# Moving the second transposed unit of the next batch's rows from the middle of a step to its end

## The chip, the cores and the metric

The kernel runs on one core of one Trainium2 chip. The metric is the device time of one execution in microseconds, the median of the runs. TensorE (PE) multiplies and transposes through PSUM banks, VectorE (DVE) and ScalarE (ACT) read those banks and write to SBUF, GpSimd (POOL) multiplies probabilities and sends rows, and SyncE (SP) starts the other transfers. Each engine works off its own program in order. Semaphores are the only order between them.

## The reference

Four blocks are chained, each as x = x + layernorm(block(layernorm(x))), on 8 batches of 512 rows by 256 features, in f32:

- block 1: causal attention with 16 heads of 64 and a linear position bias, then an output projection;
- block 2: a matrix product with a pooled low-rank term, here folded into one weight;
- block 3: a linear attention with two key and value sets, an inner layernorm and an output projection;
- block 4: a shared gated network plus 64 experts, of which each row takes 8.

The attention of block 1 is what matters here:

```
scores = einsum('bihd,bjhd->bhij', q, k) * scale + bias      # causal, 16 heads
attn   = softmax(scores);  out = einsum('bhij,bjhd->bihd', attn, v) @ Wo + bo
```

q, k and v are products of the normalised rows of x with weights. TensorE contracts over partitions, so the normalised rows `xa` (128 rows by 256 features, four tiles) must first be transposed into `xT` (128 features by 512 rows, two chunks of features).

## The kernel before, in words

The first half of the program (to about 1140 us) goes through the batches. Batch 0 is written out, batches 1 to 6 are a hardware loop, and batch 7 is written out again. The second half does the experts and the rest.

A batch is eight steps, g = 1 to 7 and then 0. A step scores the pair of heads g, normalises its softmax, and finishes the pair before: its probabilities are transposed and multiplied with the values. It also projects q and k of the next pair. Blocks 2 to 4 of the batch before (`TENSOR_AT`, `SCALAR_AT`, `VECTOR_AT`) and the preparation of the next batch (`X_AT`, `RING_AT`) are laid into slots of these steps. Step 7 projects pair 0 of the next batch, for which it needs all of the next batch's `xT`.

The order of TensorE within a step is written out in `TENSOR_STEP`, and that of ScalarE in `SCALAR_STEP`:

```
TENSOR_STEP: P0 b S0 S1 q T00 P1 T01 T02 T10 T11 k T12 S2 O e
SCALAR_STEP: F03 F13 P0 b q E00 T00 E01 P1 T01 T02 T10 T11 k E02 T12 E10 E11 E12 O e
```

P are the projections (L1551), S the scores (L1562), T the transposes of probabilities (L1573; T11 is the second unit of the second head, T12 the third), O is the product with the values (L1587), E and F are exponentials on ScalarE (L804). b, q, k and e are the slots. O stands last but one.

P, T, O and the units of `RING_AT` share PSUM banks 4 and 5 in turn. TensorE fills one bank while ScalarE empties the other. A unit may start once the unit two turns before it has been copied out by ScalarE (`ring_free`, L1517, on semaphore `ring_ready`). T02 and T10 borrow score banks instead and take no turn. ScalarE takes the copies in the same order, waiting for each unit on `ring_psum`.

The units of `RING_AT` are V (values of the next batch, L1542), L (transposes for block 3, L1620) and X. X 0 and X 1 are the two chunks of the next batch's `xT`: four 128x128 transposes each on TensorE (L1533, which wait for the normalised rows of DVE, L1067) and one copy of 128x512 by ScalarE (`a_copy` at L788). They stand in batches 0 to 6, seven times in all.

Two orders at a slot matter. TensorE's `extras` issues the units of the slot first and then the parts of `TENSOR_AT`. ScalarE's `extras` takes the parts of `SCALAR_AT` first and then the units. At slot e of step 6 the part is `l1o_T` in both: eight transposes into banks 6 and 7 (L1610) and two copies to `xTp`. In batch 0 no such part exists. The first thing of step 7 on TensorE is P0, and for the next batch's pair it waits for the copy of X 1:

```
if nxt[1] == 0:
    pe.wait_ge(ring_ready, ring_count(a, ("X", 1)))
projection(a, ("P", g, int(part[1])), nxt[1], int(part[1]))
```

The first copy of O goes to `oT`, those of T to `pT`. All of them are made by the helper at L788, so the rows tell them apart by what they write.

Of the kernel before, what the change touches and what calls it, by code (L numbers as in the profile page):

```python
# [79 lines left out]
def bass_sandwich(nc, x, wq, wk, wv, wo, bo, ffn_w, ffn_d, l1_wq, l1_wqT, l1_bq, l1_wk, l1_bk, l1_wv, l1_bv,  # L80
# [12 lines left out]
    with ctx:  # L93
# [184 lines left out]
        def score_banks(hp, u):  # L278
# [16 lines left out]


        RING_AT = {(1, 'b'): (('V', 4),), (1, 'k'): (('V', 5),), (3, 'k'): (('V', 6),), (4, 'b'): (('V', 7),), (5,
                   'k'): (('L', 0),), (6, 'b'): (('L', 1),), (6, 'k'): (('X', 0), ('X', 1)), (7, 'k'): (('V', 0), ('V',
                   1)), (7, 'e'): (('V', 2),), (0, 'e'): (('V', 3),)}
        EARLY_RING = (("X", 0), ("X", 1), ("P", 0, 0), ("P", 0, 1), ("V", 0), ("V", 1), ("P", 1, 0), ("V", 2),  # L300
                      ("P", 1, 1), ("V", 3))
# [1734 lines left out]
```

How the kernel before makes its waits and increments, by code:

```python
        @block.sync  # L463
# [20 lines left out]
                for dst, src in ((a_q[:, :, D], l1_bq), (lng_c[:], ln_g), (lnb_c[:], ln_b)):  # L484
                    sp.dma_start(dst, src.rearrange("(c p) -> p c", p=P)).then_inc(post_loaded, 16)
            def load_xs(a):
                sp.wait_ge(xs_used, at(a, 1, 0))
                sp.dma_start(xs[:], x_v[index(a)]).then_inc(xs_loaded, 16)
            load_xs((None, 1))
            sp.wait_ge(setup_made, N_MADE)
            slots_v = disp.rearrange("(e c) w -> c e w", c=CAP)
            for rows, t in ((slots_v[0:P], 0), (slots_v[P:CAP], 1)):
                n = rows.shape[0]
# [8 lines left out]
            def batch_out(p):  # L506
                sp.wait_ge(x3_ready, at(p, 1, 1))
                sp.dma_start(x3_d[index(p)], x2[:].rearrange("p t d -> p (t d)")).then_inc(batch_stores, 16)
                sp.wait_ge(xTp_ready, at(p, C * ROUNDS, C * ROUNDS))
                sp.dma_start(hT_d[index(p)], hT[:].rearrange("p c n -> p (c n)")).then_inc(batch_stores, 16)
                sp.wait_ge(batch_stores, at(p, 32, 32))
                sp.sem_inc(stored, 1)
# [1 line left out]
            def next_x(a, p):  # L515
                sp.wait_ge(x1_used, at(p, 1, 1))
                sp.dma_start(x1[:], x_v[index(a)]).then_inc(x1_loaded, 16)
# [17 lines left out]
            last = (None, B - 1)
            sp.wait_ge(ring_psum, ring_count(last, ("P", HP - 2, 1)))
            for n in range(3):
# [10 lines left out]
                load_w1(e, e)  # L550
                load_w2(e, e)
            sp.wait_ge(x1_used, B)
            load_early(EARLY - 1)
```

## Time and profile before

| | us |
|---|---|
| median of 3 runs | 2179.06 |
| the three runs | 2185.43, 2179.06, 2171.68 |
| profiled execution, its time | 2178.4 |
| profiled execution, its span | 2176.3 |
| TensorE busy in the span | 2081.0 (96%) |
| ScalarE busy | 825.8 (38%) |
| VectorE busy | 941.5 (43%) |
| GpSimd busy | 846.0 (39%) |
| mean granted clock of TensorE | 0.98 |

The span runs from the first to the last instruction. A granted clock of 1.00 is 2.4 GHz and 0.50 is 1.2 GHz. "Idle before" in a row is the time for which the engine did nothing before the group, with the engine and line that ended it; "issue" and "remote" mean that the profile shows no engine that did.

### The profile page before, as it was taken

The numbers are of one execution on the slowest core, as the hardware profiler recorded it, in microseconds if no ns is written. First come the engines' busy times: TensorE is split into PE (matmuls) and PEld (weight loads), VectorE is DVE, ScalarE is ACT, GpSimd is POOL, SyncE is SP. The second block draws the span as 40 slices with busy tenths as digits, with TensorE's granted clock in tenths as the row PEclk, the third lists the DMA queues.
The fourth block names the chain that finished last, engine by engine and source line by source line (L and its number), as shares of the span: only waits on it lengthen the run. The fifth ranks groups of instructions, "written<-read, shape, count | busy, mean of one in ns | idle before, by whom it ended". The sixth has DMA issues, their size and how long they took to land.

```text
span 2176.3 us, 37551 instructions
## 1 busy us (share of the span) xinstructions
PE 2081.0 (96%) x11788; PEld 1540.6 (71%) x11788; DVE 941.5 (43%) x3719; ACT 825.8 (38%) x2130; POOL 846.0 (39%) x958
## 2 busy tenths in 40 slices
PE   9999999999999999999999699799999999999998
PEld 4565565565655655655666466399999999999956
DVE  3436564565564665655656324022222222222236
ACT  5756556545555465555564011111111111111110
POOL 3427436447265265274472503203222232222232
PEclk9999999999999999999999799799999999999999
DMA  6800001000000000000004000078878778778841
GB/s 211 232 1 11 11 31 66 34 22 26 31 22 10 31 16 11 23 20 13 16 29 182 24 10 32 21 273 264 262 267 269 254 264 274 263 251 276 290 107 65
DMA packets 101726, 245.65 MB, mean 113 GB/s; under 512 B 22412, under 2 KB 78187, under 8 KB 93240
## 3 DMA queue, kind: packets, MB, share of 16 engines
q1 hardware_dynamic: 75448, 224.09, 28.4%
q0 software_dynamic: 26112, 19.55, 5.6%
q8 instruction: 80, 1.31, 0.2%
q14 instruction: 86, 0.70, 0.1%
HBM read 193.97 MB, written 87.91 MB: 130 GB/s over the span
## 4 chain that ended last, share of the span: by engine, by line
PE 86%; another core or an unknown queue 4%; ACT 3%; issue 3%; DVE 2%; POOL 0%; DMA 0%; ACTq 0%; SPq 0%; DVEq 0%; POOLq 0%
PE bank L1944 19%; PE bank L1957 10%; PE bank L1551 9%; PE bank L1597 8%; PE bank L1562 6%; PE bank L1587 6%; PE bank L1851 6%; PE bank L1573 5%; PE bank L1542 5%; PE bank L1863 3%; ACT pT L788 1%; PE bank L1646 1%; ACT prob L804 1%; PE bank L1610 1%
## 5 line engine op out<-in xcount | busy, mean ns | idle before, releaser
L681 POOL TENSOR_TENSOR prob<-prob,rsum 128x512 f32<-128x512 f32 (+3 forms) x512 | 350.5, 716 | 514.0 <-DVE rsum L1094 512.0
L1944 PE MATMUL bank<-pT,big_w 128*128 128x160 f32 x3072 | 438.2, 299 | 0.0
L1944 PEld LDWEIGHTS bank<-pT,big_w 128*128 128x128 f32 x3072 | 422.7, 190 | 0.1
L687 POOL DMA_INDIRECT disp<-send,slot x288 | 287.8, 999 | 211.9 <-DVE slot L1271 124.8
L804 ACT ACTIVATE prob<-prob,negmax 128x512 f32<-128x512 f32 (+3 forms) x512 | 284.1, 562 | 86.3 <-DVE negmax L1085 75.7
L733 POOL DMA_INDIRECT acc<-qk,token_e x64 | 99.2, 1549 | 511.8 <-issue 168.5
L1085 DVE CUSTOM_DVE_ANT_0 prob<-bank,bias 128x512 f32<-128x512 f32 (+3 forms) x512 | 220.8, 487 | 143.5 <-PE bank L1562 127.9
L960 ACT ACTIVATE pT<-bank 128x480 f32<-128x480 f32 x128 | 73.1, 571 | 458.7 <-PE bank L1944 450.0
L1551 PE MATMUL bank<-xT,big_w 128*128 128x512 f32 x512 | 244.3, 599 | 1.3 <-DVE xT L1312 0.9
L1414 DVE TENSOR_TENSOR pT<-pT,bank 128x480 f32<-128x480 f32 x128 | 83.8, 655 | 335.8 <-PE bank L1944 321.6
L788 ACT ACTIVATE pT<-bank 128x512 f32<-128x512 f32 (+1 forms) x384 | 182.4, 532 | 108.9 <-PE bank L1573 71.0
L1957 PE MATMUL bank<-pT,big_w 128*128 128x160 f32 x1536 | 219.2, 299 | 0.0
L1957 PEld LDWEIGHTS bank<-pT,big_w 128*128 128x128 f32 x1536 | 210.6, 190 | 0.0
L1573 PEld LDWEIGHTS bank<-ident,prob 128*128 128x128 f32 x1280 | 146.6, 141 | 65.7 <-issue 38.0
L1573 PE MATMUL bank<-ident,prob 128*128 128x128 f32 x1280 | 172.9, 276 | 8.4 <-ACT xT L788 4.0
L1562 PE MATMUL bank<-qk 64*128 64x512 f32 (+3 forms) x1024 | 175.7, 461 | 0.0
L1587 PE MATMUL bank<-pT,v_s 128*64 128x512 f32 (+3 forms) x1024 | 162.3, 459 | 9.5 <-ACT pT L788 6.5
L1562 PEld LDWEIGHTS bank<-qk 64*128 64x128 f32 x1024 | 89.0, 188 | 98.2 <-issue 73.9
L1551 PEld LDWEIGHTS bank<-xT,big_w 128*128 128x128 f32 x512 | 88.3, 190 | 79.8 <-issue 77.4
L1587 PEld LDWEIGHTS bank<-pT,v_s 128*64 128x64 f32 x1024 | 66.9, 142 | 99.5 <-issue 67.0
L788 ACT ACTIVATE v_s<-bank 128x512 f32<-128x512 f32 x74 | 44.0, 598 | 205.3 <-PE bank L1542 96.5
L1542 PE MATMUL bank<-big_w,xT 128*128 128x512 f32 x256 | 120.8, 599 | 0.4 <-ACT oT L788 0.3
(197 smaller groups left out, 2439.9 us busy)
## 6 DMA issues: line engine op xcount, KB each, us to landing
big_w<-ew SPq DMA_DIRECT2D x64, 1536.0 KB
big_w<-ew SPq DMA_DIRECT2D x64, 768.0 KB
disp<-send SPq DMA_DIRECT2D x1, 10272.0 KB, 39.4
xT<-disp SPq DMA_DIRECT2D x64, 160.5 KB
disp<-send,slot POOLq DMA_INDIRECT x288
x<-x SPq DMA_DIRECT2D x8, 512.0 KB
x_d<-x SPq DMA_DIRECT2D x8, 512.0 KB, 2.7
hT_d<-hT SPq DMA_DIRECT2D x8, 512.0 KB, 2.6
```

The source lines that it names most:

```text
L681: i = g.tensor_tensor(pr, pr, rsum[:, n, j:T].rearrange("p (t a) -> p t a", a=1).to_broadcast([P, T - j, P]), ALU.mult)
L687: g.indirect_dma_start(out=disp, out_offset=bass.IndirectOffsetOnAxis(ap=slot[:, t, k:k + 1], axis=0), in_=send[:, t, :], in_offset=None, ...
L788: return a.activation(dst, src, ACT.Copy)
L804: a.activation(prob_rows(n, t), prob_rows(n, t), ACT.Exp, bias=negmax[:, n, t:t + 1], scale=-1.0, accum_out=psumm[:, n, t:t + 1]).then_inc ...
L1085: v.tensor_tensor_reduce(out=prob_rows(n, t), in0=blocks_of(bank[score_banks(hp, u)[s]][:, col:col + COLS[t]]), in1=blocks_of(bias[:, N - ...
L1542: ins = mm(ring_bank(a, key)[:], xT[:, c, m % T * P:(m % T + 1) * P], wv_s[:, c, m // T * 512:(m // T + 1) * 512], start=(c == 0), stop=(c ...
L1551: ins = mm(ring_bank(a, key)[:], w[:, c, hp * P:(hp + 1) * P], xT[:, c], start=(c == 0), stop=(c == C - 1))
L1562: ins = mm(bank[score_banks(hp, u)[s]][:, col:col + COLS[t]], qT[half, hp % 2, t * P:(t + 1) * P], kT[half, hp % 2, 0:COLS[t]], start=True ...
L1573: ins = nc.tensor.transpose(ring_bank(a, key)[:, col + (t - j) * P:col + (t - j + 1) * P], prob[:, n % 4, j, t * P:(t + 1) * P], ident[:])
L1587: ins = mm(dst[s * DH:(s + 1) * DH, j * P:N], v_s[:, j, (2 * hp + s) * DH:(2 * hp + s + 1) * DH], pT[:, s, T_AT[j]:T_AT[j] + N - j * P], s ...
L1944: i = mm(bank[2 * half + 1 - part][:, q * CAP:(q + 1) * CAP], w1[:, c, f * P:(f + 1) * P], xbT[:, c], start=(c == 0), stop=(c == C - 1), s ...
L1957: i = mm(bank[(4, 7)[c]][:, 0:CAP], w2[:, f, c * P:(c + 1) * P], act_e[:, f], start=(f == 0), stop=(f == FC - 1), skip_group_check=True)
```

## The change

X 1 moves from slot k of step 6, right behind X 0, to slot e of the same step. On TensorE it then stands behind T12, S2 and O and ahead of `l1o_T`. On ScalarE its copy stands behind the copy of O and the two copies of `l1o_T`. The numbers of the turns follow by themselves, since they are counted from the written orders.

```
-                   'k'): (('L', 0),), (6, 'b'): (('L', 1),), (6, 'k'): (('X', 0), ('X', 1)), (7, 'k'): (('V', 0), ('V',
+                   'k'): (('L', 0),), (6, 'b'): (('L', 1),), (6, 'k'): (('X', 0),), (6, 'e'): (('X', 1),), (7, 'k'): (('V', 0), ('V',
                    1)), (7, 'e'): (('V', 2),), (0, 'e'): (('V', 3),)}
```

## Rows read from the trace of the kernel before

**Rows 1.** Waits of PE from 140 to 1100 us: total, times, longest.

```profile
PE bank L1533 <- issue: 13.5, 5, 2.7
...
PE bank L1533 <- ACT pT L788: 4.1, 1, 4.1
PE bank L1573 <- ACT xT L788: 4.0, 5, 0.8
```

**Rows 2.** Timeline, fifth loop batch, step 6: start, length, engine, line, [idle before].

```profile
842.28 1.36 ACT L788 ACTIVATE pT<-bank 128x512 f32<-128x512 f32 x3
...
843.12 0.60 PE L1533 MATMUL bank<-ident,xa 128*128 128x128 f32 x4
...
844.11 1.90 DVE L1116 TENSOR_SCALAR xn<-bank,mv,rstd 128x256 f32<-128x256 f32 x4
...
845.76 0.60 ACT L788 ACTIVATE pT<-bank 128x512 f32<-128x512 f32 x1 [2.12 <-remote]
846.41 0.66 PE L1533 MATMUL bank<-ident,xa 128*128 128x128 f32 x4 [2.70 <-issue]
847.26 1.09 ACT L788 ACTIVATE xT<-bank 128x512 f32<-128x512 f32 x2 [0.90 <-PE bank L1533]
847.91 0.44 PE L1573 MATMUL bank<-ident,prob 128*128 128x128 f32 x2 [0.84 <-ACT xT L788]
...
848.28 0.88 PE L1562 MATMUL bank<-qk 64*128 64x256 f32 x4
848.62 0.38 ACT L788 ACTIVATE pT<-bank 128x256 f32<-128x256 f32 x1
...
849.09 3.84 PE L1587 MATMUL bank<-pT,v_s 128*64 128x512 f32 x16
```

**Rows 3.** The same, the end of the step.

```profile
852.86 1.09 PE L1610 MATMUL bank<-ident,xn 128*128 128x128 f32 x8
852.98 0.60 ACT L788 ACTIVATE oT<-bank 128x512 f32<-128x512 f32 x1 [2.31 <-PE bank L1587]
853.55 1.09 ACT L788 ACTIVATE xTp<-bank 128x512 f32<-128x512 f32 x2
853.79 1.88 PE L1551 MATMUL bank<-xT,big_w 128*128 128x512 f32 x4
...
855.49 5.47 POOL L681 TENSOR_TENSOR prob<-prob,rsum 128x512 f32<-128x512 f32 x8 [9.36 <-DVE rsum L1094]
861.09 0.60 PE L1573 MATMUL bank<-ident,prob 128*128 128x128 f32 x4
```

**Rows 4.** Timeline of PE in batch 0, the same step.

```profile
100.23 0.60 PE L1533 MATMUL bank<-ident,xa 128*128 128x128 f32 x4
101.39 0.63 PE L1533 MATMUL bank<-ident,xa 128*128 128x128 f32 x4 [0.56 <-ACT pT L788]
...
102.85 2.37 PE L1587 MATMUL bank<-pT,v_s 128*64 128x512 f32 x16
105.15 1.98 PE L1551 MATMUL bank<-xT,big_w 128*128 128x512 f32 x4
```

**Rows 5.** Windows: stretch, its length, PE busy, granted clock, DMA share, GB/s.

```profile
848.50:849.00 0.50, 0.50 (x4) 0.68 0.00 0
852.00:852.50 0.50, 0.50 (x8) 0.91 0.00 0
695.00:695.50 0.50, 0.50 (x4) 0.58 0.06 1
701.50:702.00 0.50, 0.50 (x6) 0.59 0.00 0
480.00:481.00 1.00, 0.00 (x0) 1.00 0.00 0
```

**Rows 6.** Timeline of PE, third loop batch, step 3: the wait after which 1.00 stayed.

```profile
481.91 3.72 PE L1597 MATMUL bank<-weff,xTp 128*128 128x256 f32 x16 [2.08 <-ACT xTp L788]
```

**Rows 7.** DMA queues from 840 to 847 us: packets, MB, share.

```profile
q14 instruction: 1, 0.01, 0.3%
```

## The prediction

> **What bounds the kernel now.** The busy table comes first: TensorE works in 96% of the span, every other engine in under half. An edit counts only by what it does to TensorE's queue, and the search is for its idle time. The waits of TensorE over the batches name one place above all [rows 1]: the transposes of the X pair wait 13.5 us in five pieces and 4.1 us in a sixth, and T12 waits 4.0 us for copies of X. That is one event for each of the six loop batches.
>
> The timeline of step 6 shows it from inside [rows 2]. X 0 is transposed at 843.12. X 1 follows only at 846.41, after 2.70 us idle. Its bank is the one that T11 used, and ScalarE starts the copy of T11 at 845.76 and ends it at 846.36, 0.05 us before X 1. ScalarE itself had done nothing for 2.12 us, and the row names no engine that held it. One packet of the instruction queue is in this stretch [rows 7], so I read the pause as ScalarE waiting for its own code. In batch 0, written out, the same place costs 0.56 us [rows 4].
>
> T12 at 847.91 waits again, 0.84 us, for the copy of X 0, whose bank it takes; the scores S2 and O follow at 848.28 and 849.09 [rows 2]. O takes 3.84 us where batch 0 has 2.30 (102.85 to 105.15) [rows 4], because the granted clock falls: a mean of 0.68 in 848.5 to 849.0 puts the fall from 2.4 to 1.2 GHz at 848.68, and 0.91 in 852.0 to 852.5 the return at 852.09 [rows 5]. In another batch it goes from 695.08 to 701.91 (0.58 and 0.59 in those two half microseconds) [rows 5].
>
> **The change, part by part.** Four transposes and one copy move; nothing is added or removed, and the numbers of waits and of instructions stay the same on each engine. No DMA is issued by the moved unit. SP and POOL have no part in slot k or e of this step.
>
> *The big wait (L1533, 2.70 us).* ScalarE's program up to the copy of T11 is the old one. Its pause stays where it is. T12 now stands in the place of X 1 and takes the bank two turns behind, which is again T11's. So T12 starts at 846.41 instead, and the 2.70 us change their owner and nothing else. Worth: 0.
>
> *Ahead of O.* After T12 come S2 0.37 later (848.28 minus 847.91) and O 0.81 after that: 847.59. But O takes the bank of X 0, so O waits for that copy. It started at 847.26, with 0.90 us idle before it. The row names the transposes of X 1 as what ended that idle time, though the copy of X 0 needs X 0 alone; the trace doesn't show what it waited for. If it is late by itself, it ends at 847.86 and O starts at 847.91. If it would follow T11's copy at once, O is free at 847.59. I take 847.91, the measured end. O gains 849.09 - 847.91 = 1.18 us; the other end is 1.50. T12's own copy (0.38 us) stands behind one exponential and ends about 848.9, and O reads it last, over 1.5 us into its work, so it is hidden.
>
> *Behind O.* X 1 adds its own transposes back: in 853.79 - 852.86 = 0.93 us the engine passes eight of them, so four are 0.46 us. Its rows are ready (xa was made before X 0), and so are those of `l1o_T`, made by 846.01 [rows 2]; both stand behind work that ends later.
>
> *The new wait.* P0 of step 7 needs the copy of X 1, and ScalarE has three copies ahead of it. Count from the point where O lets the next unit start, 852.86 before [rows 3]. X 1 fills 0 to 0.46, `l1o_T` 0.46 to 1.39, and TensorE is free for P0 at 1.39. ScalarE copies O from 0.12, the first half of `l1o_T` from about 1.1 (four transposes last 0.60), the second from 1.6 (its transposes end at 1.39 plus some 0.16). X 1 follows after 0.49 and takes 0.60: end at 2.69, P0 at 2.74. P0 started at 0.93. It moves by 1.81 us, of which 0.46 is X 1 and 1.35 idle. Queued behind P0 are S0, S1 and `l1wo`, so nothing fills the idle time. Net for a loop batch: 1.81 - 1.18 = +0.63 us.
>
> *ScalarE and POOL.* The exponentials of step 7 start 0.5 us later. POOL then needs 5.47 us from 855.49 for both heads, while T00 is reached at 861.09 [rows 3]. It needs only the first unit, a matter of one or two us: 3 us to spare, so nothing is lost.
>
> *Batch 0.* No `l1o_T`, no pause. T12 takes X 1's start at 101.39 and everything to O is 0.46 us sooner. Behind O, X 1 fills 0.46 us, the copies of O and X 1 end at about 0.12 + 0.49 + 0.60 = 1.2 us and P0 starts at 1.25 instead of 0. Net +0.8 us.
>
> Sum at an unchanged clock: 6 x 0.63 + 0.8 = **+4.6 us**.
>
> *The clock.* Low stretches like 848.68 to 852.09 cost about 3.84 - 2.30 = 1.5 us; long ones, as from 695.08, about 2.7 (half of 6.83 us, less the idle parts in it). Three of each make 12.6 us. The falls follow the idle time at X. A wait of 2.08 us, from 479.83, saw the clock stay at 1.00 [rows 5, 6]; 2.70 plus 0.84 us, with 0.66 us of work between, was. The first gap stays, and the second shrinks from 0.84 to 0.32 us, with dense work beginning 1.2 us sooner. So the event lies between the two rows, nearer to the one with the fall. I take that a third of the cost goes, 4.2 us; the ends are 0 and 12.6 saved. The new idle time at P0 could also lengthen a low stretch: up to three short ones would turn long, 3 x 1.2 = 3.6 us lost.
>
> The Trainium skill ("TensorE: Matmul & The Clock Gate", section "HAM oscillation — how this bites in real kernels") says that the clock falls after gaps during which the array waits, and that the cure is to take the gaps out. By that rule alone the falls stay, because 2.70 us stay in one piece, and the sum would be +4.6.
>
> In total: +4.6 - 4.2 = +0.4 us on the profiled 2178.4, so 2178.8. That execution lies 0.7 us below the median of the runs, 2179.06, so I write 2179.4 for the median to come.
>
> **The rivals.**
>
> *A: as above, the wait inherited, a new one at P0, part of the clock back.* 2179.4; its own range is 2170 to 2188. For it: the turn order, which gives T12 the bank of T11. Chance 0.70.
>
> *B: the clock doesn't fall any more.* The gap before dense work is 1.2 us shorter. 4.6 - 12.6 = -8, and with O at its early start another 6 x 0.32 = 1.9 less: 2169 to 2171. Against it: the 2.70 us alone exceed the 2.08 of rows 6. Chance 0.13.
>
> *C: the pause goes with the X pair.* If what holds ScalarE at T11's copy hangs on the two X units standing together, all of it goes: 2.14 us in five batches and 3.56 in the one with 4.12 (each against 0.56 in batch 0), 14.3 us, and the falls of the clock with it, 12.6: 4.6 - 26.9 = -22, 2157, just over 1% faster. For it: the row names nothing that held ScalarE, and the 0.90 us before the copy of X 0 are named after X 1. Against it: T11's copy stands ahead of both and waits for neither. Chance 0.06.
>
> The Trainium skill ("Runtime: NRT & Kernel Launch", section "Instruction fetch mechanics") holds that crossing into a new block of code is mostly hidden, which would speak against my reading of the pause and for C. The packet in the stretch and the 2.12 us beside it [rows 2, 7] say that here it isn't hidden, so C gets little.
>
> *D: slower, the pause lands in the new wait.* P0 now waits for the fourth of four copies in a row. If ScalarE's next pause, of 2.12 us as in rows 2 or more, falls between the copies of `l1o_T` and X 1, P0 stands for it in full: 6 x 2.12 = 12.7, and a low clock behind it 6 x 1.5 = 9: 4.6 + 21.7 = +26, 2205. It decides where a pause of over 1.4 us lies within those two instructions. For it: pauses of ScalarE with no named cause come back in the same place of every loop batch, and this chain had no slack on them before. Against it: in rows 3 the copies run back to back. Chance 0.06.
>
> *E: nothing changes,* since the clock and P0 cancel otherwise than I think or the banks change hands without effect: 2176 to 2182. Chance 0.05.
>
> **How the numbers follow.** The likeliest case gives 2179.4. The range takes in A with its bounds and B: 2167 to 2190, with one or two us at each end for the scatter of the runs, which spread from 2171.68 to 2185.43. C and D lie outside. A change of 1%, 22 us, is what can be told from none here. C is mostly beyond it and D too: faster 0.06, slower 0.06, within 1% 0.88.
>
> **What the next profile would show.** In step 6: X 0, then an idle time of about 2.7 us in front of T12 (L1573) and not of L1533; O starting about 1.2 us sooner behind X 0 than before; X 1 between O and `l1o_T`; and in step 7 L1551 idle for about 1.35 us, ended by ScalarE's copy to `xT`, six times, and once shorter in batch 0. The granted clock falls in four or fewer of the six batches, or for shorter. I am wrong on the main step if T12 doesn't wait, or if ScalarE's 2.12 us stand elsewhere; on the size, if the idle time at P0 is under 1 or over 2 us.

## The result, and the profile after

| | before | after |
|---|---|---|
| median of six runs each, us | 2175.66 | 2186.03 |
| lowest to highest, us | 2171.68 to 2185.43 | 2181.15 to 2193.47 |
| ratio after to before, 95% interval | | 1.0038 [1.0023, 1.0054] |
| profiled execution, us (span) | 2178.4 (2176.3) | 2193.5 (2191.4) |
| mean granted clock | 0.980 | 0.979 |

The change makes the kernel slower by 0.4%, about 8 to 10 us. That is inside the range and within 1%, but it is not the +0.4 us of the forecast. The profiled execution after is the longest of its six runs, so its whole difference of 15 us is not the change's. In the second set below, one execution each of e5, e6 and the kernel before took 4115 to 5202 us; the medians of that set count it, and the ratios leave it out.

The waits of PE from 140 to 1100 us come first, as in [rows 1]: total, times, longest.

```profile
PE bank L1573 <- issue: 10.7, 4, 3.4
...
PE bank L1573 <- ACT pT L788: 8.7, 3, 4.1
PE bank L1551 <- ACT xT L788: 7.8, 6, 1.3
```

L1533, which headed [rows 1] with 13.5 and 4.1 us, is gone from the list. L1573, where T12 stands, now has the long waits. New is L1551, the projection P0 of step 7: six times 1.3 us, all for the copy to `xT`.

The timeline of the fifth loop batch, step 6, answers to [rows 2, 3] (start, length, engine, line, [idle before]).

```profile
851.70 0.60 PE L1533 MATMUL bank<-ident,xa 128*128 128x128 f32 x4
...
855.76 0.60 ACT L788 ACTIVATE pT<-bank 128x512 f32<-128x512 f32 x1 [3.54 <-remote]
856.25 0.59 ACT L788 ACTIVATE xT<-bank 128x512 f32<-128x512 f32 x1
856.41 0.69 PE L1573 MATMUL bank<-ident,prob 128*128 128x128 f32 x2 [4.11 <-ACT pT L788]
857.03 1.22 PE L1562 MATMUL bank<-qk 64*128 64x256 f32 x4
...
858.18 4.52 PE L1587 MATMUL bank<-pT,v_s 128*64 128x512 f32 x16
862.63 0.66 PE L1533 MATMUL bank<-ident,xa 128*128 128x128 f32 x4
862.75 0.60 ACT L788 ACTIVATE oT<-bank 128x512 f32<-128x512 f32 x1 [3.55 <-PE bank L1587]
863.12 1.04 PE L1610 MATMUL bank<-ident,xn 128*128 128x128 f32 x8
863.76 1.08 ACT L788 ACTIVATE xTp<-bank 128x512 f32<-128x512 f32 x2 [0.41 <-PE bank L1610]
864.73 0.60 ACT L788 ACTIVATE xT<-bank 128x512 f32<-128x512 f32 x1
865.46 1.98 PE L1551 MATMUL bank<-xT,big_w 128*128 128x512 f32 x4 [1.30 <-ACT xT L788]
```

The order is the predicted one: X 0, idle, T12, S2, O, X 1, `l1o_T`, idle, P0. At the end ScalarE makes four copies (O, then 0.41 us later `l1o_T` twice and X 1 back to back, until 865.33), and P0 waits 1.30 us for the fourth. The pause ahead of T11's copy is there too. It is 3.54 us in this batch and 2.08 us in the second loop batch, whose timeline follows. There X 0's copy comes late by itself as well (0.90 us).

```profile
391.92 0.60 PE L1533 MATMUL bank<-ident,xa 128*128 128x128 f32 x4
...
394.53 0.60 ACT L788 ACTIVATE pT<-bank 128x512 f32<-128x512 f32 x1 [2.08 <-remote]
395.18 0.69 PE L1573 MATMUL bank<-ident,prob 128*128 128x128 f32 x2 [2.66 <-issue]
...
396.03 0.60 ACT L788 ACTIVATE xT<-bank 128x512 f32<-128x512 f32 x1 [0.90 <-PE bank L1573]
396.96 4.53 PE L1587 MATMUL bank<-pT,v_s 128*64 128x512 f32 x16
```

Batch 0, the timeline of PE, answers to [rows 4].

```profile
100.82 0.60 PE L1533 MATMUL bank<-ident,xa 128*128 128x128 f32 x4
101.98 0.41 PE L1573 MATMUL bank<-ident,prob 128*128 128x128 f32 x2 [0.56 <-ACT pT L788]
...
105.25 0.66 PE L1533 MATMUL bank<-ident,xa 128*128 128x128 f32 x4
106.60 1.98 PE L1551 MATMUL bank<-xT,big_w 128*128 128x512 f32 x4 [0.69 <-ACT xT L788]
```

The windows answer to [rows 5] (stretch, length, PE busy, clock, DMA share, GB/s): the start of the low clock in the second loop batch, its first and last half microsecond in the fifth, and the start of one in block 2 that the kernel before did not have.

```profile
394.50:395.00 0.50, 0.00 (x0) 0.93 0.00 0
855.50:856.00 0.50, 0.00 (x0) 0.73 0.00 0
862.50:863.00 0.50, 0.50 (x5) 0.95 0.00 0
637.00:637.50 0.50, 0.20 (x1) 0.77 0.00 0
```

The clock goes from 2.4 to 1.2 GHz still inside the first wait, at 855.73, and is back at 862.55. It falls in all six loop batches, in four of them inside the first wait.

### The profile page after: what moved, and what is told of

Read it like the earlier page. It is cut to its first block, busy times and chain, and to the rows that moved or that the text cites. A ratio compares the mean times of both kernels' runs of the same rounds, so it can differ in the third digit from the quotient of the medians.

```text
span 2191.4 us, 37557 instructions
## 1 busy us (share of the span) xinstructions
PE 2086.4 (95%) x11788; PEld 1543.4 (70%) x11788; DVE 939.6 (43%) x3719; ACT 824.9 (38%) x2130; POOL 845.0 (39%) x958
## 3 DMA queue, kind: packets, MB, share of 16 engines
q1 hardware_dynamic: 75448, 224.09, 28.4%
q8 instruction: 80, 1.31, 0.3%
## 4 chain that ended last, share of the span: by engine, by line
PE 82%; another core or an unknown queue 5%; ACT 4%; issue 4%; DVE 3%; POOL 1%; DMA 1%; ACTq 0%; SPq 0%; DVEq 0%; POOLq 0%
PE bank L1944 19%; PE bank L1957 10%; PE bank L1597 9%; PE bank L1551 8%; PE bank L1851 6%; PE bank L1562 6%; PE bank L1587 5%; PE bank L1542 5%; PE bank L1573 5%; PE bank L1863 3%; ACT pT L788 2%; ACT prob L804 2%; PE bank L1646 1%; PE bank L1610 1%
## 5 line engine op out<-in xcount | busy, mean ns | idle before, releaser
L1944 PE MATMUL bank<-pT,big_w 128*128 128x160 f32 x3072 | 438.2, 299 | 0.0
L1944 PEld LDWEIGHTS bank<-pT,big_w 128*128 128x128 f32 x3072 | 422.7, 190 | 0.1
L804 ACT ACTIVATE prob<-prob,negmax 128x512 f32<-128x512 f32 (+3 forms) x512 | 283.9, 561 | 85.1 <-DVE negmax L1085 74.9
L1551 PE MATMUL bank<-xT,big_w 128*128 128x512 f32 x512 | 245.0, 600 | 10.5 <-ACT xT L788 8.5
L1573 PEld LDWEIGHTS bank<-ident,prob 128*128 128x128 f32 x1280 | 146.6, 141 | 81.0 <-issue 50.5
L1573 PE MATMUL bank<-ident,prob 128*128 128x128 f32 x1280 | 173.2, 276 | 23.4 <-issue 10.7
L1551 PEld LDWEIGHTS bank<-xT,big_w 128*128 128x128 f32 x512 | 88.1, 190 | 90.6 <-issue 77.0
```

The costliest lines, as they stand in the source:

```text
L804: a.activation(prob_rows(n, t), prob_rows(n, t), ACT.Exp, bias=negmax[:, n, t:t + 1], scale=-1.0, accum_out=psumm[:, n, t:t + 1]).then_inc ...
L1551: ins = mm(ring_bank(a, key)[:], w[:, c, hp * P:(hp + 1) * P], xT[:, c], start=(c == 0), stop=(c == C - 1))
L1573: ins = nc.tensor.transpose(ring_bank(a, key)[:, col + (t - j) * P:col + (t - j + 1) * P], prob[:, n % 4, j, t * P:(t + 1) * P], ident[:])
L1944: i = mm(bank[2 * half + 1 - part][:, q * CAP:(q + 1) * CAP], w1[:, c, f * P:(f + 1) * P], xbT[:, c], start=(c == 0), stop=(c == C - 1), s ...
```

## The experiments

Three sets ran against the kernel before in the same runs. Its median was 2194.63 us in the first set (e1 to e4), 2176.45 in the second (e5 to e8) and 2073.69 in the third (e9 to e11), on three different chips, and 2073.69 again beside e12, on a fourth. What that difference shows stands at the end.

**e1: the changed kernel, with ScalarE's copy ahead of `l1o_T`'s.**

```
+    units = ring_units(g, slot, p is not None, following is not None)
+    if (g, slot) == (6, 'e'):
+        for key in units:
+            ring_evac(a_, key)
+        units = []
```

> X 1 stays at slot e as in the changed kernel, but ScalarE takes its copy ahead of the two copies of l1o_T. Theory (the new wait at P0 is a cost of the change): ScalarE's copy of X 1 ends about 0.3 us before TensorE is free for P0, the idle time before L1551 (1.30 us, six times) goes, and the time falls by 6 x 1.30 = 7.8 us against the changed kernel: ratio to before 1.000 where the changed one has 1.0038. Rival (the loss comes from ScalarE's longer pauses and from the clock, and the wait at P0 is absorbed later): the idle time before L1551 goes, but the ratio stays near 1.004.

Measured: 2193.32 us, ratio 0.9994 [0.9984, 1.0004]. The waits of PE, same stretch (the lines lie five further down: L1578 is T, L1592 is O, and L1556, P0, waits for no copy to `xT`):

```profile
PE bank L1578 <- ACT pT L788: 21.1, 5, 4.3
```

With the copy two places earlier the wait at P0 is gone in the loop (0.69 us stay in batch 0), and with it the loss. T12 keeps its waits. So the 0.4% is the order of the copies on ScalarE. The move on TensorE is by itself worth 0.16% at most, the lower end of this interval, and may be worth nothing.

**e2: both X units at slot e, copies first.**

```
-  (6, 'k'): (('X', 0), ('X', 1)),
+  (6, 'e'): (('X', 0), ('X', 1)),
```

with the lines of e1.

> Both X units stand at slot e, ScalarE copies them ahead of l1o_T. No unit of X stands between T11 and T12, so T12 takes the other bank and doesn't wait for T11's copy. Theory (the turn order decides who inherits ScalarE's pause): T12 and S2 run during the pause, O waits for T11's copy, idle about 1.6 to 1.9 us instead of 2.7 plus 0.84, O starts 2.7 us earlier than before, X 0 and X 1 add 0.92 us behind it: 6 x -1.76 = -10.6 us, ratio to before 0.995; if the shorter idle time also keeps the clock at 2.4 GHz, another 12 us, ratio 0.990. Rival (what is won in step 6 is lost at P0, which now waits for two copies): ratio 1.000 or above, with L1551 idle for over 1.5 us.

Measured: 2190.89 us, ratio 0.9981 [0.9969, 0.9993]. O now stands where X 1 and T12 did. The timeline of the first loop batch:

```profile
242.84 0.60 ACT L788 ACTIVATE pT<-bank 128x512 f32<-128x512 f32 x1 [3.69 <-remote]
243.49 4.53 PE L1592 MATMUL bank<-pT,v_s 128*64 128x512 f32 x16 [3.85 <-ACT pT L788]
```

The wait has a third owner, the same copy of T11 ends it, and the gain is 0.19%, well under the 0.5% that I expected. ScalarE's pause at T11's copy is up to 3.7 us long on this chip, and O still waits 2.4 to 3.9 us: 19.7 us in the six batches, where X 1 and T12 together wait 24.5 in e3, the kernel before but for 32 increments. e2 is the only kernel whose interval lies below 1.

**e3: the kernel before with 32 semaphore increments ahead of ScalarE's loop,** to shift its program against the blocks in which it is loaded.

```
+            for _ in range(32):
+                act.sem_inc(code_pad, 1)
```

> The kernel before, with 32 semaphore increments that nobody waits for put into ScalarE's program once, just before the loop over the batches (some 2 us of ScalarE's time once). Theory (the pause is ScalarE waiting for its own code, at fixed places of the program): the pause of 2.1 us leaves T11's copy and stands some 32 instructions earlier in the loop body; X 1 then waits about 0.56 us as in batch 0, not 2.70, and the clock doesn't fall there; by where the other pauses land the time moves by -25 to +15 us. Rival (the pause hangs on the X units or on a semaphore of that place): it stays in front of T11's copy with 2.1 us, and the ratio is 1.000.

Measured: 2195.95 us, ratio 1.0002 [0.9993, 1.0011]. The pause stayed at T11's copy, X 1 waiting 4.2 to 4.3 us for it in five batches and 2.84 in the sixth. The trace has the 32 increments as ScalarE's own instructions, from 133.7 to 135.8 us, so they do take places in its program. e7 and e8 put such places into the loop itself.

**e4: the kernel before with X 0's transposes done six times over,** so that TensorE works through the wait of X 1.

```
-                for t in range(T):
+                for t in [*range(T)] * (6 if c == 0 else 1):
```

> The kernel before, with the four transposes of X 0 made six times over into the same place before the unit is signalled: 20 more transposes of 0.107 us, 2.1 us of work inside the idle 2.7 us, in batches 0 to 6. Theory (the idle time at X is what lets the clock fall, and the low stretches cost about 12.6 us in all): the granted clock stays at 1.00 in all six loop batches, batch 0 loses 1.6 us, in total -11 us, ratio 0.995. Rival (the falls have another cause, or the second gap of 0.84 us is enough): the clock falls as before, ratio 1.000 to 1.001.

Measured: 2201.53 us, ratio 1.0028 [1.0017, 1.0039]. The waits of PE, same stretch:

```profile
PE bank L1551 <- issue: 10.5, 7, 2.2
...
PE bank L1533 <- ACT pT L788: 8.3, 4, 2.1
```

The wait of X 1 shrank to 0.6 to 2.1 us in each batch, and in batches 1 and 2 the clock stayed at 1.00 through step 6. In the other four it fell in step 6 all the same, at 551.7, 708.7, 865.7 and 1022.7. The one at 865.7 came behind gaps of only 0.62 and 1.02 us, and in batch 2 gaps of 0.65 and 0.99 left it at 1.00. But other projections (L1551) now wait up to 2.2 us for nothing that the profile shows, where neither the kernel before nor e3, on this same chip, has such a row among its long waits. In three batches the clock falls right there (609.5, 766.5 and 923.5). The low clock up to 1100 us lasts 23.9 us, and 37.5 in e3. So less idle time went with less low clock, but I had expected no fall at all, and the same idle time went both ways. The edit doesn't price the clock either: what it saved in step 6 came back in other places.

**e5: the changed kernel once more,** as a base for e6.

> The changed kernel as it is, on the same chip as the other three of this call and against the same runs of the kernel before. Theory: ratio 1.0035 to 1.0045, L1551 idle for 1.30 us in six batches and 0.69 us in batch 0. Rival (the 1.0038 measured first was a matter of that chip, where ScalarE's pause was 2.1 us in five batches of six before and 3.5 us in more of them after): with pauses of 3.5 us in most batches on either side the ratio is 1.000 to 1.002.

Measured: 2185.04 us, ratio 1.0031 [1.0017, 1.0046]. P0 waits 1.30 us six times and 0.69 once, to the hundredth as before. T12 waits 4.12, 2.01, 1.29, 3.42, 2.74 and 3.42 us in the six loop batches: this wait is another in each execution.

**e6: the changed kernel with two more copies ahead of X 1's,** from the same bank into a scratch tile.

```
+                    if m and a_ != "early":
+                        for k in range(2):
+                            a_copy(late[:, k], src)
```

> The changed kernel, with two more copies of the bank of X 1 (into a scratch tile that nobody reads) by ScalarE ahead of the real one. Theory (each copy ahead of X 1's own delays P0 in full): L1551 is idle for 1.30 + 2 x 0.49 = 2.28 us in six batches and 1.67 us in batch 0, and the time is 6.9 us, 0.3%, above the changed kernel of the same call. Rival (later waits take the delay up): the idle time grows, the ratio stays within 0.1% of the changed kernel's.

Measured: 2192.48 us, ratio 1.0054 [1.0038, 1.0069]. Timeline, fifth loop batch (lines one or four further down):

```profile
860.55 1.09 ACT L789 ACTIVATE xTp<-bank 128x512 f32<-128x512 f32 x2 [0.46 <-PE bank L1614]
861.52 1.09 ACT L789 ACTIVATE late<-bank 128x512 bf16<-128x512 f32 x2
862.48 0.63 ACT L789 ACTIVATE xT<-bank 128x512 f32<-128x512 f32 x1
863.24 1.98 PE L1555 MATMUL bank<-xT,big_w 128*128 128x512 f32 x4 [2.28 <-ACT xT L789]
```

Two copies of 0.49 us each put P0 back by 0.98, from 1.30 to 2.28, in all six batches. The chain from ScalarE's row of copies to P0 carries what is laid into it. Over e5 the ratio grew by 0.23%, some 5 us, and the median by 7.4, against 7 x 0.98 = 6.9 in the waits; the intervals hold either.

**e7 and e8: the kernel before with 16 or 32 register instructions** at the head of ScalarE's loop body, each with a wait that is already met.

```
+                for n in range(16):
+                    act.wait_ge(biased, at((b, 1), H * T, -16 - n))
```

> The kernel before, with 16 register instructions at the head of the loop body of ScalarE, each with a wait that is long fulfilled; every later instruction of the body stands 16 places further on. Theory (ScalarE's pause is the arrival of a block of its code at a fixed place): the pause leaves T11's copy and stands 16 instructions earlier, some 8 operations, about at the copy of k or T00's in step 6; X 1 waits for less than 1 us; by where the pauses land the time moves by up to 25 us, down rather than up. Rival (the pause hangs on that operation or on what TensorE does there): it stays in front of T11's copy, ratio 1.000.

> The same with 32 register instructions. Theory: the pauses stand 32 places earlier, near the copy of O and the exponentials between step 5 and step 6, where TensorE has the projections and scores to do; the wait at X falls to about 0.56 us. Rival: as with 16, nothing moves, ratio 1.000 to 1.001 (32 more instructions of some 0.05 us in six batches, 10 us of ScalarE's time, at a place where it has slack).

Measured: 2177.3 us, ratio 1.0000 [0.9988, 1.0013], and 2175.48 us, 0.9995 [0.9985, 1.0006]. The timeline of ScalarE in e8, fifth loop batch, and the DMA queues in two stretches of e8, 803 to 806 and 838.5 to 840 us (packets, MB, share):

```profile
839.58 0.62 ACT L788 ACTIVATE pT<-bank 128x512 f32<-128x512 f32 x1
842.30 0.60 ACT L788 ACTIVATE pT<-bank 128x512 f32<-128x512 f32 x1 [2.11 <-remote]
843.79 1.09 ACT L788 ACTIVATE xT<-bank 128x512 f32<-128x512 f32 x2 [0.89 <-PE bank L1535]
```

```profile
q14 instruction: 1, 0.01, 0.9%
q14 instruction: 1, 0.01, 1.4%
```

Step 6 starts at 836.4 here. Before, the two packets of this queue came 17.6 us ahead of the step's start and 3.1 us behind it. In e8 they come 32.3 us ahead and 2.9 us behind, in e7 24.7 ahead and 2.9 behind, and in e3 30.9 ahead and 2.9 behind. So the first packet moved with ScalarE's program, by 7, 13 and 15 us, and belongs to it. The one in [rows 7] did not move and belongs to something else. The pause did not move either: in e8 2.11 us ahead of T11's copy, then 0.89 ahead of X 0's. In all six loop batches of e3, e7 and e8 X 1 starts 0.05 us behind T11's copy, though the pause ahead of that copy is 0.68 to 2.91 us in e7. The instructions themselves show too: ScalarE's idle time at the loop's start, ended by the same exponential (L804), is 2.0 to 2.2 us before and 4.3 to 4.6 in e8, some 0.07 us for each of the 32. My reading of [rows 7] falls.

**e9 and e10: both kernels with GpSimd's sends laid out anew.** In the traces above, each pause of ScalarE in step 6 lies beside a run of GpSimd's indirect sends. There five steps have six sends each and the sixth two. Here the fifth has two and the sixth six, so that they lie elsewhere.

```
-        SENDS = -(-T * TOPK // (HP - 2))
+        SENDS_AT = (6, 6, 6, 6, 2, 6, 0)
-                    for j in range((g - 1) * SENDS, min(g * SENDS, T * TOPK)):
+                    for j in range(sum(SENDS_AT[:g - 1]), sum(SENDS_AT[:g])):
```

> The kernel before, with GpSimd's row sends laid out otherwise: of the six that it issues during step 6 of a batch (behind the heads of g = 5) four are moved one step on, so the steps hold 6, 6, 6, 6, 2, 6 instead of 6, 6, 6, 6, 6, 2. Theory (ScalarE's pauses go with a run of GpSimd's sends: in the trace of before they begin some 5 us after the first send of a run and end 2.0 to 2.2 us after a late one): the pause in front of T11's copy in step 6 is gone, X 1 waits 0.56 us as in batch 0, the clock doesn't fall there, and step 7 gets a pause instead; step 6 gains about 5 us six times, step 7 may give back up to 3 us each: ratio 0.987 to 0.996. Rival (the pause belongs to the place in step 6): it stays in front of T11's copy with 2.1 to 3.6 us, ratio 0.999 to 1.001.

> The changed kernel with the same new layout of the sends. Theory: T12 waits 0.56 us as in batch 0, the idle time at P0 of step 7 stays at 1.30 us, and against the kernel of the run before this one the change costs what it costs without any pause: in batch 0 it was 4.92 to 5.78 us from X 0 to P0, with l1o_T behind it 0.8 to 1.3 us per batch, 6 to 9 us in all, 0.3 to 0.4%. Rival (the change gains once the pause is gone, since O is no longer behind a late copy): equal or faster than the run before this one.

Measured: 2073.98 us, ratio 0.9999 [0.9990, 1.0008], and 2083.98 us, 1.0047 [1.0033, 1.0060]. On this chip the kernel before takes 2073.69 with its sends as they were, so the sends explain nothing of the 100 us. But the granted clock is 1.00 in both, ScalarE has no pause at these places, and the pair isolates the change. The packet of [rows 7] is in e9 as well, 2.4 us behind the start of step 6, and nothing pauses at it. The timeline of e10, fifth loop batch:

```profile
809.04 0.60 PE L1533 MATMUL bank<-ident,xa 128*128 128x128 f32 x4
...
810.10 0.44 PE L1573 MATMUL bank<-ident,prob 128*128 128x128 f32 x2 [0.47 <-ACT pT L788]
811.10 2.37 PE L1587 MATMUL bank<-pT,v_s 128*64 128x512 f32 x16
813.41 0.65 PE L1533 MATMUL bank<-ident,xa 128*128 128x128 f32 x4
...
814.54 1.08 ACT L788 ACTIVATE xTp<-bank 128x512 f32<-128x512 f32 x2 [0.42 <-PE bank L1610]
815.51 0.60 ACT L788 ACTIVATE xT<-bank 128x512 f32<-128x512 f32 x1
816.24 1.98 PE L1551 MATMUL bank<-xT,big_w 128*128 128x512 f32 x4 [1.30 <-ACT xT L788]
```

The wait at T12 is 0.47 us, as X 1's was in e9. The wait at P0 is the same 1.30. From the start of step 6 to P0 of step 7 a loop batch takes 9.04 us in e9 and 10.45 in e10, and batch 0 8.17 and 9.02. That is 6 x 1.41 + 0.85 = 9.3 us of the 10.0 measured. With no pause and no fall of the clock, nothing comes back.

**e11: both X units at slot e, copies first (e2), with 7, 7, 6, 6, 2 and 4 sends.**

> Both X units at slot e with ScalarE's copies ahead of l1o_T (the second experiment), and sends laid out 7, 7, 6, 6, 2, 4. Theory: no pause in step 6, no idle time at P0 in the loop batches, only short runs of sends in steps 6 and 7: the fastest of all, ratio 0.985 to 0.992. Rival (seven sends in a run lengthen the pauses of steps 2 and 3 and give it back): 0.994 to 0.998.

Measured: 2073.49 us, ratio 0.9997 [0.9988, 1.0006]. Step 6 to P0 takes 8.80 us in the loop, 0.24 less than in e9, and 8.87 in batch 0, 0.70 more. That comes to 0.7 us saved in all, far less than the interval.

**e12: e9 again,** for a chip on which ScalarE pauses.

> The kernel before with the row sends laid out 6, 6, 6, 6, 2, 6, once more, in the hope of a chip on which ScalarE pauses (the kernel before took 2174 to 2195 us there, and 2074 us on the one where it doesn't pause). Theory on such a chip (the pauses go with runs of GpSimd's sends): none in front of T11's copy in step 6, one in step 7 instead, ratio 0.987 to 0.996. Rival: the pause stays at T11's copy with 2.1 to 3.7 us, ratio 1.000. On a chip without pauses both say 1.000, and nothing is told apart.

Measured: 2074.17 us, ratio 1.0001 [0.9992, 1.0010], again on a chip without pauses. Whether the sends move a pause stays untested.

## Why the prediction came out as it did

*The wait is inherited: right.* It went from X 1 to T12 in the changed kernel and to O in e2. Whoever waits starts 0.05 us behind the end of T11's copy in every loop batch of these traces, also where the row says "issue". Rival C, that the pause goes with the X pair, is refuted by all of these. Rival B did not come either: the clock fell in six loop batches after, and in five of six in e5.

*The new wait: right, and it is the whole result.* Predicted 1.35 us in the loop and 0.8 in batch 0 (P0 at 1.25, of it 0.46 X 1). Measured 1.30 and 0.69, 8.5 us together. e1 takes it away and the ratio goes to 0.9994, e6 lengthens it and the ratio goes up, and e10 has it alone.

The stretch from X 0's start to P0, over the seven batches, splits as follows (idle and work of PE, summed from the two profiled executions):

| us | before | after | measured | predicted |
|---|---|---|---|---|
| idle ahead of O | 22.15 | 20.97 | -1.2 | -3.1 (6 x 0.52) |
| idle at P0 | 0 | 8.49 | +8.5 | +8.9 |
| work, with what the clock does to it | 50.43 | 52.02 | +1.6 | -5.4 (-4.2 and 6 x -0.2) |
| sum | 72.58 | 81.48 | +8.9 | +0.4 |

The 0.2 is X 1, which took 0.66 us ahead of O and 0.46 behind it. The new wait came as forecast. What the forecast set against it, a gain ahead of O and a third of the low clock, came only in part and not at all: the net of a loop batch was to be +0.63 us at an unchanged clock, and was +1.34 in these two traces.

*The clock: wrong, and it is the step that failed.* I took a third of 12.6 us as saved, because the event would lie between [rows 6] and the fall. After the change the clock fell in all six batches. In four of them it fell inside the first gap, as in the second loop batch in the half microsecond from 394.50, before T12 began at 395.18; what came behind the gap could save nothing there. In the third it fell at 548.53, inside O's wait of 1.14 us, with one of 1.95 before it. In the fourth it fell at 705.54, 0.66 us into O, behind waits of 2.69 and 0.42. From O's start to the next unit of TensorE the six batches took 25.3 us in all, and 22.9 before: O lay under the low clock for longer, not for shorter.

The trace before had shown that the first gap, which the change leaves alone, is enough. In its fourth loop batch the clock fell at 695.08 [rows 5], behind this gap and ahead of the second one, which T12 ends at 696.25:

```profile
694.77 0.87 PE L1533 MATMUL bank<-ident,xa 128*128 128x128 f32 x4 [2.72 <-issue]
```
The low time also changes from one execution to the next. Up to 1100 us it is 30.7 in the profiled execution before, 30.7 in e7 and 23.9 in e8, which are the same kernel but for the register instructions. It is 41.0 after, of which 34.1 belong to step 6 and 6.8 to two stretches outside it such as the one at 637, and 23.9 in e5. A term of 4 us can be neither shown nor refuted by one pair of traces here. All five together show no saving of a third: step 6 has 29.0 us of low clock as the mean of the two traces of the changed kernel, and 28.4 as that of the three of the kernel before. I should have put the term at nothing.

The rule that I had set beside it, in the Trainium skill ("TensorE: Matmul & The Clock Gate", section "HAM oscillation — how this bites in real kernels"), speaks of gaps longer than 2.70 us. That the falls stay here as long as the gaps do was my own step from it. This mostly held: six falls of six, and five of six in e5, where the clock stayed at 1.00 through a gap of 3.42 us in the sixth loop batch. The sum with the falls unchanged was +4.6.

*The gain ahead of O: half right.* 1.18 us a batch was worked out for a low clock that begins behind T12. X 0's copy followed T11's at once in the fifth batch (856.25), as at the other end that I gave, and O did not wait. But T12, S2 and the gap to O then took 1.77 us instead of 1.18, at 1.2 GHz. In the second loop batch X 0's copy was late by itself, as I had it. Over the six batches O starts 0.99 us sooner behind X 0, with pauses that differ between the two traces. Without pauses the gain is 0.49 (5.81 to 5.32 from the step's start, e9 and e10).

*The pause of 2.12 us as a constant: wrong.* The waits that it makes were 4.12 once and 2.7 five times before. They were 3.36, 2.66, 1.95, 2.69, 4.11 and 4.08 after, and lay between 1.29 and 4.12 in e5. Much of the difference of -1.2 from -3.1 us ahead of O is this scatter.

*The pause as ScalarE's code: wrong,* by e3, e7 and e8. It changed no number of the sum, since I left the pause where it was. The Trainium skill ("Runtime: NRT & Kernel Launch", section "Instruction fetch mechanics") calls the crossing into a new block mostly hidden. I put the packet in the stretch above that, and e3, e7 and e8 show that the packet does not follow ScalarE's program. Since the pause doesn't either, no run here speaks against the Trainium skill on this.

*Rival D, the pause lands in the new wait: did not come.* P0's wait is 1.30 or 1.31 us in all twelve loop batches of the two traces. *POOL's slack in step 7: held.* L1573's waits for POOL are three of at most 0.3 us.

What holds ScalarE is open. On the chips with pauses those of step 6 lie beside a run of GpSimd's sends. In e9 sends run too, and nothing pauses, so the sends alone don't do it. That the chip decides, and not something else that differed between the sets, is not shown beyond the two sets with pauses and the two without.

## What to carry to other kernels

When a unit moves to another slot, write out the order on the engine that consumes it too: here TensorE issues the units of a slot first and ScalarE copies them last, and three copies of 0.5 to 0.6 us stood between the moved unit and the work that waits for it. A wait for a shared bank stays at its place in the queue, whoever stands there, so moving the waiting unit away does not remove it. A gain that hangs on the granted clock needs several profiled executions before it goes into a sum.

## What the runs showed of the hardware

The same kernel takes 2073.69, 2073.69, 2176.45 and 2194.63 us on four chips. On the fastest the granted clock is 1.00, and PE's waits from 140 to 1100 us come to 4.7 us. These are all that e9, the kernel before but for its sends, has:

```profile
PE bank L1533 <- ACT pT L788: 2.8, 6, 0.5
PE bank L1573 <- POOL prob L681: 1.4, 5, 0.3
PE bank L1573 <- ACT pT L788: 0.3, 1, 0.3
PE bank L1587 <- ACT pT L788: 0.2, 1, 0.2
```

On the other two, and in the traces before and after, ScalarE stands still for up to 5.6 us at a time, in every loop batch, with no engine named, and the clock falls behind some of these. PE's waits in the same stretch come to 41.1 us before and 55.5 in e3.

ScalarE's pauses are not all of it. The spans before and in e9 are 2176.3 and 2071.4 us. The first product at L1851, behind the batches, starts at 1181.3 and 1122.7 us, and the first at L1944 at 1413.2 and 1308.3, so 46 of the 105 us arise between these two points. There TensorE itself stands still ahead of single products with nothing named, in rows that e9 doesn't have, while GpSimd's sends run in both. The clock is low for 51 us of it in two stretches (0.52 and 0.51 as means from 1220 to 1245 and from 1364 to 1392). The waits of PE in the trace before, from 1100 to 1500 us:

```profile
PE bank L1863 <- issue: 15.2, 11, 2.2
PE bank L1851 <- issue: 11.8, 11, 1.8
```

So 5% hangs on a cause that isn't in the program and that holds more than one engine, and the change that was tried here moves 0.4%.

The length of an idle gap doesn't settle by itself whether the clock falls. It fell within a single gap of PE of 2.66 us (second loop batch after), while 2.08 us in [rows 6] left it at 1.00, and so did 3.42 us in the sixth loop batch of e5, whose row and window are these:

```profile
1001.57 0.44 PE L1573 MATMUL bank<-ident,prob 128*128 128x128 f32 x2 [3.42 <-issue]
998.00:1004.00 6.00, 2.58 (x16) 1.00 0.03 3
```
